# A four-layer graph network on Trainium2: gathers that check bounds and skip the rows that a step does not use

## What is computed

```
layer 0: up = h @ W_up; tpw = mlp(edge_attr_16); m = products of tpw, up[src], edge_attr_4
         msg = segment_sum(m, dst);  node-wise polynomial, linear maps, normalisation
layer 1: sums = segment_sum((h @ W_src)[src], dst) / deg;  + h, batch norm, relu
layer 2: xp = h @ W;  alpha = leaky_relu(a_src[src] + a_dst[dst] + a_edge)
         attn = softmax of alpha over the edges of a receiver, 8 heads
         out = segment_sum(xp[src] * attn, dst) + bias;  layer norm
layer 3: as layer 2, without a_edge
```

## Time and profile before

| | |
|---|---|
| median of 3 runs | 5649.62 us (5645.04 to 5650.47) |
| span of the profiled execution | 5646.4 us |
| its instructions | 88904 |
| PE, DVE, ACT, POOL busy | 70%, 72%, 53%, 63% |
| mean granted TensorE clock | 0.830 of full speed |
| gathers from POOL in the four passes | 4 x 880 |
| software DMA queue q0 (POOL's) | 173552 packets, 491.76 MB, 30.5% of 16 engines |

### The profile page before, as it was taken

How to read it: one execution, slowest core, us unless ns; L and a number is a source line. 1 busy time by engine, 2 the same in 40 slices (tenths; PEclk the granted TensorE clock), 3 DMA queues, 4 the chain that set the end, 5 groups by cost and what they waited for, 6 DMA issues and landing times. The chain is left out here.

```text
span 5646.4 us, 88904 instructions
## 1 busy us (share of the span) xinstructions
PE 3948.6 (70%) x21347; PEld 3074.9 (54%) x21348; DVE 4045.3 (72%) x9134; ACT 2966.6 (53%) x8448; POOL 3558.8 (63%) x3592
## 2 busy tenths in 40 slices
PE   5799999999776666666674555555575565555566
PEld 3577777777564555555553544444533455555552
DVE  4799999999753333333376888888876788888887
ACT  4799999999444444444353333333343333333331
POOL 2577777777106777777706777777701777777760
PEclk9899999999888888888786777777787777777777
DMA  8444444444214545555324555555502555555543
GB/s 262 113 97 99 99 98 98 98 99 98 68 37 133 135 135 135 135 135 135 112 92 143 145 145 143 143 145 145 145 17 78 144 144 144 143 141 142 143 115 95
DMA packets 693374, 687.48 MB, mean 122 GB/s; under 512 B 458792, under 2 KB 561755, under 8 KB 691471
## 3 DMA queue, kind: packets, MB, share of 16 engines
q0 software_dynamic: 173552, 491.76, 30.5%
q1 hardware_dynamic: 378451, 164.47, 11.6%
q10 hardware_dynamic: 141276, 30.14, 2.8%
HBM read 627.87 MB, written 57.66 MB: 121 GB/s over the span
## 5 line engine op out<-in xcount | busy, mean ns | idle before, releaser
L1875 POOL DMA_INDIRECT g3rows<-sender_rows,g3idx x880 | 843.4, 958 | 525.6 <-issue 265.0
L1109 POOL DMA_INDIRECT c0rows<-rows,c0idx x880 | 994.7, 1130 | 285.1 <-issue 270.8
L878 POOL DMA_INDIRECT g1rows<-rows,g1idx x880 | 832.0, 945 | 541.5 <-DMA g1idx<-src_of 273.8
L1875 POOL DMA_INDIRECT g2rows<-sender_rows,g2idx x880 | 842.1, 957 | 412.0 <-issue 282.9
L1138 ACT ACTIVATE c0z<-c0rows,c0sh 128x128 f32<-128x128 f32 x2640 | 795.4, 407 | 1.6 <-DVE c0prod L1305 1.6
L999 DVE TENSOR_TENSOR acc<-acc,g1psA 128x258 f32 x660 | 279.7, 424 | 720.9 <-PE g1psA L904 568.1
L907 PE MATMUL g1psA<-g1rows,g1sel 128*128 128x129 f32 x2640 | 472.1, 346 | 359.2 <-DMA g1rows<-rows,g1idx 321.2
L907 PEld LDWEIGHTS g1psA<-g1rows,g1sel 128*128 128x128 f32 x2640 | 452.7, 257 | 402.5 <-issue 350.2
L1909 PE MATMUL g3psA<-g3rows,g3sel 128*128 128x136 f32 x2640 | 442.8, 327 | 153.8 <-DVE g3rows L2087 102.4
L1230 PE MATMUL c0psA<-c0prod,c0sel 128*128 128x256 f32 x1760 | 547.3, 393 | 3.5 <-DVE acc L1319 3.5
L1909 PE MATMUL g2psA<-g2rows,g2sel 128*128 128x132 f32 x2640 | 439.6, 328 | 154.5 <-DVE g2rows L2087 102.3
(11 more groups left out here) (420 smaller groups left out, 8759.5 us busy)
## 6 DMA issues: line engine op xcount, KB each, us to landing
g2bc<-dst_rows SPq DMA_DIRECT2D x55, 512.0 KB, 4.0
g3bc<-dst_rows SPq DMA_DIRECT2D x55, 512.0 KB
g1f<-in_edge_attr SPq DMA_DIRECT2D x103, 256.0 KB, 3.5
c0rows<-rows,c0idx POOLq DMA_INDIRECT x880, 2.8
g1rows<-rows,g1idx POOLq DMA_INDIRECT x880
g2rows<-sender_rows,g2idx POOLq DMA_INDIRECT x880
g3rows<-sender_rows,g3idx POOLq DMA_INDIRECT x880
rbf_steps<-prep_extra POOLq DMA_DIRECT2D x7, 1024.0 KB, 10.8
```

The costliest lines, as they stand in the source:

```text
L878: g.indirect_dma_start(rows[b][:, u, 0:D], None, k.table, bass.IndirectOffsetOnAxis(ap=idx[b][:, u:u + 1], axis=0)).then_inc(r_sem[b], 16)
L1109: g.indirect_dma_start(rows[b][:, m, place(n), :], None, k.table, bass.IndirectOffsetOnAxis(ap=idx[b][:, 4 * m + n:4 * m + n + 1], axis=0) ...
L1875: g.indirect_dma_start(rows[b][:, u, 0:TW], None, k.sender_rows, bass.IndirectOffsetOnAxis(ap=idx[b][:, u:u + 1], axis=0)).then_inc(gas[b] ...
```

## The change

The indices of edges that their step does not use are raised by 16384, which is above the last row of every table (NP - 1 = 6271). All gathers of the four passes carry `bounds_check=NP - 1, oob_is_err=False`: a row with an index above the bound is skipped and the buffer keeps what it held. So that a buffer never holds anything but finite numbers, DVE writes all row buffers once at the start of each pass (zeros, in `aggregate` ones), and the first gather into each buffer waits for that. With 880 x 128 = 112640 indices and 106250 edges, each used once, 6390 indices are out of bounds, 5.67%. They lie in the 96 steps of straddled tiles, about half of each, in the padded end of the last tile and in the unused step. The other steps, some 780, have none.

```diff
+SKIP = float(1 << 14)
...
             v.wait_ge(S["gr"], 16 * Z)
-            nc.vector.tensor_copy(srcf[:, :, :], srci[:, :, :]).then_inc(S["gs"], 1)
+            step(nc.vector.tensor_copy(srcf[:, :, :], srci[:, :, :]))
+            step(nc.vector.tensor_scalar(npen[:, :, 0:P], rel[:, :, :], 0.0, SKIP, ALU.is_lt, ALU.mult))
+            step(nc.vector.tensor_tensor(srcf[:, :, :], srcf[:, :, :], npen[:, :, 0:P], ALU.add))
+            step(nc.vector.tensor_scalar(npen[:, :, 0:P], rel[:, :, :], float(P), SKIP, ALU.is_ge, ALU.mult))
+            nc.vector.tensor_tensor(srcf[:, :, :], srcf[:, :, :], npen[:, :, 0:P], ALU.add).then_inc(S["gs"], 1)
+            v.wait_ge(S["gs"], 1)
...
                 g.wait_ge(i_sem[b], n * 16 + 16)
+                if not later(n):
+                    g.wait_ge(S["cl"], b + 1)
...
                     g.indirect_dma_start(rows[b][:, u, 0:D], None, k.table,
-                                         bass.IndirectOffsetOnAxis(ap=idx[b][:, u:u + 1], axis=0)
-                                         ).then_inc(r_sem[b], 16)
+                                         bass.IndirectOffsetOnAxis(ap=idx[b][:, u:u + 1], axis=0),
+                                         bounds_check=NP - 1, oob_is_err=False).then_inc(r_sem[b], 16)
...
             for b in range(4):
-                nc.vector.memset(rows[b][:, :, D:], 1.0).then_inc(S["cl"], 1)
+                nc.vector.memset(rows[b][:, :, :], 1.0).then_inc(S["cl"], 1)
...
+            for b in range(2):
+                nc.vector.memset(rows[b][:, :, :, :], 0.0).then_inc(S["rc"], 1)
             nc.vector.memset(k.acc[:, :, 0:D], 0.0).then_inc(S["cl"], 1)
...
+            for b in range(3):
+                nc.vector.memset(rows[b][:, :, :], 0.0).then_inc(S["rc"], 1)
             for t_ in (tb, of):
```

More of the change, by code:

```diff
@@ L1015, in convolve @@
     names = ["idx0", "idx1", "lr0", "lr1", "ls0", "ls1", "w", "wf", "sel", "z", "sk", "y", "x", "msg", "mm", "acc",
-             "rt", "rx", "m1", "a1", "m2", "a2", "m3", "a3", "tp", "cl", "go"]
+             "rt", "rx", "m1", "a1", "m2", "a2", "m3", "a3", "tp", "cl", "go", "rc"]
     gats = ["gat00", "gat01", "gat10", "gat11"]
@@ L1102, in gather @@
                 g.wait_ge(i_sem[b], i * 16 + 16)
+                if not later(i):
+                    g.wait_ge(S["rc"], b + 1)
                 for m in range(2):
@@ L1109, in gather @@
                         g.indirect_dma_start(rows[b][:, m, place(n), :], None, k.table,
-                                             bass.IndirectOffsetOnAxis(ap=idx[b][:, 4 * m + n:4 * m + n + 1], axis=0)
-                                             ).then_inc(g_sem[b][m], 16)
+                                             bass.IndirectOffsetOnAxis(ap=idx[b][:, 4 * m + n:4 * m + n + 1], axis=0),
+                                             bounds_check=NP - 1, oob_is_err=False).then_inc(g_sem[b][m], 16)
             pairs(g, NBC, gather)
@@ L1777, in gat @@
              "init", "oh", "z", "zt", "loc", "q0", "q1", "q2", "lev", "arg", "rt", "al", "rs", "d", "dt", "w",
-             "msg", "sel", "acc", "c", "v", "mx", "go", "sp"]
+             "msg", "sel", "acc", "c", "v", "mx", "go", "sp", "rc"]
     es, s = scope(nc, [tag + n for n in names], [(tag + f"ga{b}", k.gathered.pop()) for b in range(3)])
@@ L1875, in gather @@
                     g.indirect_dma_start(rows[b][:, u, 0:TW], None, k.sender_rows,
-                                         bass.IndirectOffsetOnAxis(ap=idx[b][:, u:u + 1], axis=0)
-                                         ).then_inc(gas[b], 16)
+                                         bass.IndirectOffsetOnAxis(ap=idx[b][:, u:u + 1], axis=0),
+                                         bounds_check=NP - 1, oob_is_err=False).then_inc(gas[b], 16)
             triples(g, NB, gather)
```

## The result

The kernel with the change takes 5786.61 us in the median of 4 runs (5783.05 to 5791.4), and the kernel before, run beside it, 5650.05 us. The ratio is 1.0245, with a 95% interval of 1.0232 to 1.0257: 2.4% slower, or 136.6 us.

The account below looks back on a forecast made before the run. Three passes were taken as bound by POOL's gather issue rate, c0 by PE, DVE and ACT. 5646.4 + 8.8 (start-up) + 185 (gathers) = 5840 us, plus 3.2 us to the median: 5844 us, range 5560 to 6330 us.

Parts of the forecast that it names:

- The bound: Passes g1, g2 and g3, some 3350 us of 5646, go at the rate at which POOL issues gathers.
- 0.03 us above the bare rate: In g2 and g3 gathers start 1.279 and 1.280 us apart, against 1.250 us in g1, where POOL never waits.
- The sign: Gathers of g1, g2 and g3: the check outweighs the saving, so the kernel gets slower; chance 0.57.
- the asymmetry: In the gathers, the check touches every row and the saving one row in 18; break-even needs a check under 6%.
- if POOL must still write something for it, nothing: Lower bound on the saving per gather from skipped rows: zero if POOL still writes an entry for each.
- The size: Per gather in g1, g2 and g3: check 0.09 us less saving 0.02 us, net +0.07 us, x 2640 = +185 us.
- the sharing out of the 0.37 us: POOL's extra time for an indirect over a direct transfer, put on 128 indices at 2.9 ns each.
- c0: Pass c0: PE, DVE and ACT full, 0.2 us of slack per gather, so no gain or loss from gathers: 0.
- The start-up terms: Prepare 3.6 us, clears in c0 3.4 us, in g1 0, in g2 and g3 1.8 us; together 8.8 us.
- No stall beside clears: Gathers beside DVE's clears stay at 0.95 us, so no stall charged; the skill's rule would give some 10 us a pass.
- The faster rival: Gathers: check free, skipped rows save; by bytes 0.017 us per gather, 5613 us; chance of the faster case 0.29.

## Why the prediction was right, and where it was off

- **The bound** was read rightly: three passes at the pace of POOL's gathers. All of 52 ns per gather arrived, 138.8 us for 2640 of them. In g2 and g3 the "0.03 us above the bare rate" was left without a reason. In g2 it is 15.5 us of waiting for PE ahead of the tenth gather of each batch and some 10 us of gathers held up beside DVE. There POOL does wait, so the 46.8 us of g2 are 50.1 us more of gathers less 3.3 us of idle time.
- **The sign** rested on the asymmetry that the check touches every row and the saving one in 18. It held more strongly than put: the saving is none at all. The bound given as "if POOL must still write something for it, nothing" is the one that holds, and the 4 bytes of a skipped row fit it.
- **The size** of the term was off. The check was taken at 0.09 us and measured 0.052 us; the saving was taken at 0.02 us and measured 0. The net of 0.07 us gave 185 us, where 139 us came. The step that failed is the sharing out of the 0.37 us between an indirect and a direct transfer over 128 indices. It gave 2.9 ns per index where 0.73 ns was measured. The difference between the two kinds of instruction is mostly fixed, if the line through 64 and 128 lanes goes on below, and a fourth of it was no measure for a comparison. No run shows a part of 0.09 us. What the check measured is 24 ns for the gather and 0.22 ns for an index. The total came out near partly by luck, since the two errors offset each other. With the check at 0.09 us and the true saving of 0 the sum would have held 238 us for the gathers instead of 185 us.
- **c0** was expected to neither lose nor gain. It had the slack for 52 ns, as said. That it would gain 9 us was not among the cases: I had read the stretched gathers as a reserve and not as a sign that POOL and DVE hold each other up.
- **The start-up terms** were taken as 8.8 us and measured as 11.8 us (6 to 16). The comparison in prepare runs at 1.09 us and not at 0.63 us, and the clears of c0 cost some 4.3 us instead of 3.4 us with the gaps between them. For g2 the first gather starts 4.45 us after the first clear does, 0.87 us behind its end, where I had charged the clear's end and no step behind it. The timelines of DVE and POOL with the change:

```profile
3028.06 3.58 DVE L2007 MEMSET g2rows<- 128x4224 f32 x1 [3.07 <-PEq L81]
```

```profile
3032.51 1.01 POOL L1889 DMA_INDIRECT g2rows<-sender_rows,g2idx  x1 [130.03 <-DVE g2rows L2007]
```

- **No stall beside clears** held, as the timelines of POOL and DVE at the start of g1 with the change show:

```profile
1717.52 0.99 POOL L886 DMA_INDIRECT g1rows<-rows,g1idx  x1 [0.30 <-issue]
...
1722.72 1.00 POOL L886 DMA_INDIRECT g1rows<-rows,g1idx  x1 [0.30 <-issue]
```

```profile
1717.62 1.78 DVE L979 MEMSET g1rows<- 128x2064 f32 x1 [0.38 <-issue]
1721.98 10.59 DVE L980 MEMSET acc<- 128x12642 f32 x1 [2.58 <-issue]
```

  Neither beside the clears of 1.78 us nor beside the one of 10.59 us does a gather take longer. The rule of the Trainium skill ("SBUF — State Buffer", the box on "DVE blocks DMA") is about DVE instructions in a two-port mode. No trace here shows in which mode an instruction runs. So the prediction's word that the trace agrees with the rule in c0 said more than the rows did. What they show is that gathers are held beside L1277 and L1302 in c0 and beside the bf16 comparison in g2, and not beside a clear.
- The sum of what was measured is 138.8 - 8.6 + 11.8 = 142 us, against 136.6 us between the two kernels. The difference of 5.4 us is about what the start-up term is uncertain by (6 to 16 us).
- **The faster rival** by bytes, with the page "DMA: Bandwidth & Descriptors" of the Trainium skill, fell. With 95% of the bytes of that queue gone the gathers of g1 still started 1.302 us apart.

## What to carry to other kernels

When a pass moves at the pace at which POOL issues gathers, its price is the number of gather instructions, hardly the rows and not the bytes: about 1.25 us each here, of which the rows of 64 lanes make up 47 ns. Marking rows to be skipped saves traffic and costs POOL time. By that it would pay only where the DMA queues bind and POOL does not, and a gain here would have to come from fewer gathers; neither was tried. And where POOL's gathers run beside DVE's SBUF work, a change of 50 ns in one of them moved the whole pass by 0.7% in c0, and another moment of landing went with 0.8% to 0.9% in g2, in either direction. Such a pass is measured and not counted.

## What the runs showed of the hardware

- A gather of 128 rows keeps POOL busy for 0.946 us, of 64 rows for 0.899 us; 0.305 us pass until the next. Checking bounds adds 52 ns (38 ns at 64 rows) when out of bounds is skipped and 66 ns when it is an error, with every index in bounds.
- A skipped row leaves the packets of the queue unchanged (173552 with none, 6390 of a pass's 112640, over half or all rows skipped) and takes all of its bytes but 4 (491.76, 465.28, 245.13 and 24.98 MB).
- With no row fetched, the first consumer in g2 starts 1.30 us behind the end of a batch's last gather; with over half of the rows skipped 1.75 us and with 5.67% skipped 2.02 us.
- A gather that starts inside DVE's L1277 or L1302 of c0 (fp32, two SBUF operands) is held, and ends 0.81 to 0.83 us behind the end of that instruction (267 gathers in the kernel before, typically 1.56 and 1.61 us long). Beside DVE's bf16 comparison in g2 it is held as well (1.46 us). Inside L1295, with one operand in PSUM (71 gathers, 0.940 to 0.948 us), and beside fp32 clears it is not.
- A gather that starts within 12 ns of DVE's L1297, L1298 or L1305 in c0 adds 0.05 us to DVE's time there (198 meetings in the kernel before); 50 ns earlier or later it does not (L1297).
